# A transformer layer in fp32 on one core: the feed-forward taken for 512 tokens at once

## What is computed

```python
qkv = x @ Wqkv + bqkv                                # 256 -> 3 x 256
att = softmax(where(causal, q @ k.T * 16**-0.5, -inf))
x = layernorm(x + (att @ v) @ Wout + bout)
h = silu(x @ w1.T * w1_s) * (x @ w2.T * w2_s)        # 256 -> 1024
h = gelu(h @ h1.T * h1_s)                            # 1024 -> 1024
h = gelu(h @ h2.T * h2_s)                            # 1024 -> 1024
out = layernorm(x + h @ w3.T * w3_s)                 # 1024 -> 256
```

## Time and profile before

| what | value |
|---|---|
| median of 3 runs | 2513.91 us (2510.92 to 2515.61) |
| the profiled execution | 2513.84 us |
| its span, first to last instruction | 2512.1 us |
| TensorE busy | 2366.4 us (94%) |
| VectorE busy | 1264.6 us (50%) |
| ScalarE busy | 1335.7 us (53%) |
| GpSimd busy | 487.7 us (19%) |
| DMA moved | 183.35 MB, mean 73 GB/s |
| mean granted TensorE clock | 0.959 |

### The profile page before, as it was taken

How to read it: one execution, slowest core, us unless ns; L and a number is a source line. 1 busy time by engine, 2 the same in 40 slices (tenths; PEclk the granted TensorE clock), 3 DMA queues, 4 the chain that set the end, 5 groups by cost and what they waited for, 6 DMA issues and landing times.

```text
span 2512.1 us, 53072 instructions
## 1 busy us (share of the span) xinstructions
PE 2366.4 (94%) x16550; PEld 1834.4 (73%) x16550; DVE 1264.6 (50%) x3961; ACT 1335.7 (53%) x3104; POOL 487.7 (19%) x894
## 2 busy tenths in 40 slices
PE   5667999999999999999999999999999999999988
PEld 2225777777777777777777777777777777778788
DVE  2364454555545555554555555455555544555433
ACT  1334645555564655556465555646555564656543
POOL 0112212221220222122022212202221220222111
PEclk7557999999999999999999999999999999999999
DMA  4852122122222212112221211212121121212000
GB/s 153 295 184 64 53 68 76 51 86 61 60 68 63 81 52 85 61 54 75 62 82 52 85 60 54 75 62 82 52 85 54 60 75 59 85 52 65 13 5 9
DMA packets 109284, 183.35 MB, mean 73 GB/s; under 512 B 20608, under 2 KB 38784, under 8 KB 108928
## 3 DMA queue, kind: packets, MB, share of 16 engines
q1 hardware_dynamic: 109104, 180.70, 23.2%
HBM read 109.86 MB, written 72.88 MB: 73 GB/s over the span
## 4 chain that ended last, share of the span: by engine, by line
PE 75%; issue 6%; DVE 4%; ACT 3%; POOL 3%; POOLq 0%; ACTq 0%; DVEq 0%; SPq 0%; DMA 0%
PE ring L910 40%; PE ring L896 7%; PE pS L813 6%; PE ring L923 5%; PE pO L846 5%; PE pM L824 4%; PE ring L855 3%; PE ring L861 2%; POOL Xlo L486 2%; ACT probs L519 1%; PE ring L877 1%; POOL probs L480 1%; DVE pM L647 1%; ACT L574 1%; PE ring L885 1%
## 5 line engine op out<-in xcount | busy, mean ns | idle before, releaser
L647 DVE CUSTOM_DVE_ANT_0 pM<-pM,mask 128x512 f32<-128x512 f32 (+3 forms) x1024 | 491.9, 510 | 526.3 <-PE pM L824 431.9
L519 ACT ACTIVATE probs<-pS 128x512 f32<-128x512 f32 (+3 forms) x1024 | 392.1, 434 | 291.3 <-PE pS L813 288.3
L910 PE MATMUL ring<-Xhi,H 128*128 128x256 f32 x2048 | 528.0, 297 | 19.8 <-POOL Xlo L486 13.0
L910 PE MATMUL ring<-Yhi,H 128*128 128x256 f32 x2048 | 528.5, 296 | 0.0
L910 PE MATMUL ring<-Ylo,H 128*128 128x256 f32 x2048 | 504.3, 284 | 0.0
L910 PE MATMUL ring<-Xlo,H 128*128 128x256 f32 x2048 | 499.1, 282 | 0.0
L480 POOL TENSOR_SCALAR_AFFINE_SELECT probs<-probs 128x256 f32<-128x256 f32 x512 | 211.6, 413 | 1276.3 <-ACT probs L519 1272.3
L910 PEld LDWEIGHTS ring<-Xhi,H 128*128 128x128 f32 x2048 | 390.7, 191 | 46.6 <-ACT full_h L587 14.0
L910 PEld LDWEIGHTS ring<-Yhi,H 128*128 128x128 f32 x2048 | 394.5, 193 | 34.3 <-issue 21.0
L910 PEld LDWEIGHTS ring<-Ylo,H 128*128 128x128 f32 x2048 | 395.5, 193 | 0.0
L910 PEld LDWEIGHTS ring<-Xlo,H 128*128 128x128 f32 x2048 | 391.8, 191 | 4.4 <-issue 3.4
(11 more groups left out here) (88 smaller groups left out, 3026.5 us busy)
## 6 DMA issues: line engine op xcount, KB each, us to landing
Qs<-qk_d SPq DMA_DIRECT2D x64, 512.0 KB, 3.6
Ks<-qk_d SPq DMA_DIRECT2D x64, 512.0 KB, 4.5
qk_d<-c_hi SPq DMA_DIRECT2D x64, 256.0 KB, 2.4
qk_d<-c_hi SPq DMA_DIRECT2D x128, 128.0 KB, 2.4
qk_d<-c_lo SPq DMA_DIRECT2D x128, 128.0 KB, 2.4
xTs<-in_xT SPq DMA_DIRECT2D x16, 512.0 KB, 3.8
Oc<-Osb SPq DMA_DIRECT2D x256, 32.0 KB
xr<-in_x SPq DMA_DIRECT2D x16, 512.0 KB, 5.6
```

What stands on the lines that cost most here:

```text
L519: nc.scalar.activation(probs[:, e % NP_BUF, s, 0:n], pS[:, s, 0:n], ACT.Exp, scale=SCALE).then_inc(exp_done, 1)
L647: nc.vector.tensor_tensor_reduce(pM[:, s, 0:n], pM[:, s, 0:n], mask[:, T - n:T], 1.0, NEG, ALU.add, ALU.max, mx[:, t, 2 * p + s:2 * p + s ...
L910: mm = nc.tensor.matmul(to, w, x_part, start=(k == 0 and m == 0), stop=(k == KB - 1 and m == 1))
```

## The change

- The feed-forward takes all 512 tokens of an image at once. There are 8 `gu`, 8 `h1` and 8 `h2` units an iteration in place of 16 each, and their matmuls have 512 columns. A `gu` unit takes two ring banks (m = 0 gate, m = 1 up). `ffn_out` is still done in two halves.
- Xhi, Xlo, Yhi and Ylo double in size. To make room, H2 is no longer held whole: it is written once to DRAM in eight tiles (`h2_d`) and loaded each iteration, tile by tile, into three slots (`h2_load`, 512 KB each). x1Thi and x1Tlo lie over Yhi and Ylo, th over c_hi and c_lo, xr, x1 and z become one buffer xz for two images, and full_h is gone: the second gelu is written in place in PSUM.
- The low part of the gated product goes from GpSimd to VectorE.
- The list of steps is written anew: four table loads instead of eight, `qk` of the next image in exps(2), `h2` from unit 2 on after the last head group, `y` and `ln1` at the end of the same iteration. The loop on the hardware takes two iterations at a time.
- A ring bank of an h unit is now free after VectorE's subtraction (h_lo), not after ScalarE's second gelu (h_full).

```diff
     def exps(g, between):       # unchanged: exp of kt, p; steps "between"; pv(kt - 1)
+    def gated(j):
+        return [("gu", -1, (j,)), ("ffn_hi", -1, (j,))]
+    def hidden(layer, early, after):
+        for j in range(early):
+            steps.extend([("h_act", -1, (layer, j)), ("h_rest", -1, (layer, j))])
+        for j in range(early, KB):
+            add(layer, -1, j)
+            add("h_act", -1, layer, j)
+            steps.extend(after.get(j, []))
+            add("h_rest", -1, layer, j)
+            if layer == "h2" and j + H2_BUF < KB:
+                add("h2_load", -1, j + H2_BUF)
...
+    exps(1, {0: gated(4), 1: gated(5), 2: [m[0]], 3: gated(6) + [m[1]],
+             5: gated(7) + [m[2]], 6: [m[3]]})
...
+    exps(2, {0: [("qk", 1, (0,))], 1: [n[4]], 2: [n[5], ("qk", 1, (1,))], 3: [n[6]],
+             4: [n[7], split, ("qk", 1, (2,))], 6: [turn, ("qk", 1, (3,))]})
+    last_pv(2)
+    add("h2", -1, 0)
+    m = maxes(1, 0)
+    exps(3, {1: [m[0]], 2: [m[1]], 3: [m[2]], 4: [m[3]], 5: [m[4]], 6: [m[5]]})
+    add("h2", -1, 1)
     add("table", 0, "Gelu", 3)
+    last_pv(3)
+    add("h2_load", -1, 3)
+    add("h2_load", -1, 4)
+    split, turn = neg(1, 0)
+    n = maxes(1, 1)
+    hidden("h2", 2, {2: [("v", 1, (0,)), m[6], ("den", 0, ())],
+                     3: [("v", 1, (1,)), m[7], split, ("rec_save", 0, ())],
+                     4: [("v", 1, (2,)), turn, ("rec_load", 0, ())],
+                     5: [("v", 1, (3,)), n[0]],
+                     6: [n[1], ("den_turn", 0, ())],
+                     7: [("y", 0, (0,)), n[2], ("y", 0, (1,))]})
+    add("ln1_stats", 0)
+    add("ln1", 0)
...
+                    elif kind == "h2_load":
+                        j, = a
+                        slot = j % H2_BUF
+                        if j < H2_BUF:
+                            need(sp, h_ready, (b - 1) * UNITS + KB + H2_BUF * (H2_PER[slot] - 1) + slot + 1)
...
+                        else:
+                            sp.wait_ge(h_ready, b * UNITS + KB + j - H2_BUF + 1)
+                        held(sp)
+                        sp.dma_start(H2[:, slot].bitcast(F32), h2_d[j]).then_inc(h2_in[slot], 16)
...
-                    elif kind == "ffn_hi":
-                        half, j = a
-                        pool.wait_ge(x_hi, b * (2 * KB) + half * KB + j + 1)
-                        nc.gpsimd.tensor_tensor(Xlo[:, j], full_g[:, j % 2], Xhi[:, j].bitcast(F32),
-                                                ALU.subtract).then_inc(x_lo, 1)
...
+                    elif kind == "ffn_hi":
+                        j, = a
+                        dve.wait_ge(x_hi, b * KB + j + 1)
+                        nc.vector.tensor_tensor(Xlo[:, j], full_g[:, j % 2], Xhi[:, j].bitcast(F32),
+                                                ALU.subtract).then_inc(x_lo, 1)
...
-                "gu": lambda half, j: (ffn_full, 2 * KB, half * KB + j + 1),
-                "h1": lambda half, j: (h_full, 32, u_of("h1", half, j) + 1),
-                "h2": lambda half, j: (h_full, 32, u_of("h2", half, j) + 1),
-                "ffn_out": lambda half: (ln2, LN2, 6 * half + 1),
+                "gu": lambda j, m: (gated, KB, j + 1) if m else (ffn_full, KB, j + 1),
+                "h1": lambda j: (h_lo, UNITS, u_of("h1", j) + 1),
+                "h2": lambda j: (h_lo, UNITS, u_of("h2", j) + 1),
+                "ffn_out": lambda half: (ln2[half], LN2, 2),
...
+                        if kind == "h2":
+                            pe.wait_ge(h2_in[j % H2_BUF], 16 * (b * H2_PER[j % H2_BUF] + j // H2_BUF + 1))
```

More of the change, by code:

```diff
@@ L52 @@
 VW = D + 1
-NP_BUF = 4
 MISC = 3
+H2_BUF = 3
+H2_PER = [len(range(n, KB, H2_BUF)) for n in range(H2_BUF)]
 def plan_iteration():
@@ L81, in last_pv @@
         add("stack", 0 if g + 2 < NG else 1, (g + 2) % NG)
-    def hidden(layer, off, half, g, early, after):
-        if not early:
-            last_pv(g)
-            steps.extend(after.get(-1, []))
-        for j in range(early, KB):
-            add(layer, off, half, j)
-            waiting = [(layer, half, k) for k in range(early)] if j == early else []
-            for k, unit in enumerate(waiting):
-                steps.append(("h_act", off, unit))
-                if k == 0:
-                    last_pv(g)
-            if waiting:
-                steps.append(("h_rest", off, waiting.pop(0)))
-            add("h_act", off, layer, half, j)
-            steps.extend(after.get(j, []))
-            steps.extend(("h_rest", off, unit) for unit in waiting)
-            add("h_rest", off, layer, half, j)
@@ L104, in maxes @@
     def maxes(off, g):
         return [("max", off, (g, t, p)) for t in reversed(range(TB)) for p in range(PAIRS)]
-    def gated(off, half, at, others):
-        between = {e: list(more) for e, more in others.items()}
-        for e, n in at:
-            between.setdefault(e, []).append(("gu", off, (half, n)))
-            if n:
-                between.setdefault(e + (e == 6 and n == KB - 1), []).append(("ffn_hi", off, (half, n - 1)))
-        return between
-    m = maxes(0, 1)
-    add("table", 0, "Exp", 0)
@@ new lines, in plan_iteration @@
+    add("table", 0, "Exp", 0)
+    m = maxes(0, 1)
+    split, turn = neg(0, 1)
+    exps(0, {0: [("ffn_out", -2, (0,))],
+             1: [m[3], ("x1_turn", -1, (0,)), ("x1_turn", -1, (1,))],
+             2: [m[4], ("ffn_out", -2, (1,))],
+             3: [m[5], ("ln2_stats", -2, (0,))],
+             4: [m[6]] + gated(0) + [("ln2", -2, (0,))],
+             5: [m[7], split, ("load_xT", 1, ())],
+             6: gated(1) + [turn],
+             7: gated(2)})
+    last_pv(0)
+    steps.extend(gated(3))
@@ L670, in work @@
                     elif kind == "gu":
-                        half, j = a
-                        n = b * (2 * KB) + half * KB + j
-                        gate, up = (ring[:, BANKS[kind, off, a], m * HALF:(m + 1) * HALF] for m in range(2))
+                        j, = a
+                        n = b * KB + j
+                        gate, up = (ring[:, BANKS[kind, off, (j, m)]] for m in range(2))
+                        dve.wait_ge(gu_ready, 2 * n + 2)
+                        held(dve)
                         dve.wait_ge(tanh_done, n + 1)
@@ L784, in _, with iteration @@
             }
-            def iteration(i, steps, taken, general):
+            def iteration(i, steps, odd, taken, general):
                 def bank(kind, off, a):
```

337 lines of the change are left out of this document (161 added, 176 removed).

## The result

The changed kernel takes **3253.9 us** (median of 4 runs, 3248.2 to 3263.5) against 2513.1 for the kernel before on the same chip: ratio 1.295, interval 1.291 to 1.299. I had said 2820, range 2590 to 2960. Slower was right; the size was wrong by 434 us. The profiled execution has a span of 3246.8 us.

A forecast was written before the change was run, and what follows sets the result against it. TensorE's stream bounds the kernel; per iteration 12.1 us saved against 32.6 of waits, less 1.5 already there, gives +19.0 on 147.6. Over 15 iterations +285, +20 for the ends: 2513.8 becomes 2820 us, range 2590 to 2960.

The forecast's parts named there:

- The saving of wider matmuls: In h and gu units, 512-column matmuls at 216 ns take 12.1 us off an iteration of 147.6.
- rival D: Feed-forward matmuls of 512 columns take 240 ns, +92 us: 2910 us; chance 0.18 together with rival C.
- Wait 1: In exps(2), four c_hi in one phase each wait for the save before: 10.4 us an iteration, bounds 7.9 and 12.
- Wait 2: In exps(3), first maxima wait for the next image's Qs and Ks: 7.1 us with slower maxima, bounds 3 and 8.
- Wait 3: In h2, tile 3 of H2 is loaded late, behind a group's end and a stack: 5.0 us, bounds 3.5 and 6.
- Wait 4: Before h2 units 5 and 7, ring banks come free late: 1.0 and 2.7, together 3.7 us, bounds 2 and 5.
- Wait 5: In the gated product, VectorE's pace makes h1 unit 0 wait for the last Xlo: 6.4 us, bounds 0 and 10.
- rival C: Gaps also cost clock: h2 units 0 and 1 at half clock, 7 us an iteration, 2925 us; 0.18 together with D.
- the 1.5 that I had deducted: Per iteration, 1.5 us taken off the waits since some exist already in the 135.5: +20.5 becomes +19.0.
- the ends: First iterations (qk chain twice, H2 written in 512-byte pieces) and the last one: +20 us in all.
- A: TensorE's stream decides, waits fall where it has work queued: 2320 us; 0.11 including what lies up to no change.
- B: Only the waits in exps(2) and for the next image's stack are real: 2615 us; 0.21 with what lies between.

The follow-up runs named there:

- e11: Changed kernel with each 512-column matmul of the feed-forward's first three layers as two of 256, weights loaded twice: 3293.9 us, ratio 1.311.
- e1: Changed kernel with the four qk steps spread over h1 units 2 and 5, exps(2) and exps(3): 3170.9 us, ratio 1.261.
- e9: Changed kernel with the edits of e1, e2, e3 and e6 together, plus the Qs and Ks load ahead of a group's end: 2892.0 us, ratio 1.149.
- e5: Changed kernel with unused filler matmuls: 20 before the first maxima of exps(3), 26 before h2 unit 3, 12 before unit 7: 3222.0 us, ratio 1.284.
- e2: Changed kernel with H2's tile 3 load issued behind h2 unit 0 and tile 4's ahead of group 3's end: 3152.2 us, ratio 1.254.
- e3: Changed kernel with VectorE's subtraction of an h unit ahead of the steps behind that unit: 3211.1 us, ratio 1.277.
- e6: Changed kernel with the gated product's copy Xhi and low part one unit later, as in the kernel before: 3146.7 us, ratio 1.254.
- e13: Changed kernel with unused filler matmuls at two places only, 26 before h2 unit 3 and 7 before unit 7: 3221.9 us, ratio 1.282.
- e7: Changed kernel with the gated product's low part back on GpSimd, all else the same: 3221.9 us, ratio 1.283.

## Why the prediction was wrong, point by point

**What bounds, and the direction: right.** The list before hid its waits, the new one doesn't; in each of the five places that I named the trace shows one.

**The saving of wider matmuls: mis-sized.** I took 216 ns for 512 columns from the fp32 row; bounds 213 and 240. Here they start 235 ns apart on average at 2.4 GHz (median 228, over some 3270 pairs whose next is of the same line and within 600 ns), between my value and rival D's 240. An h unit with what parts it from the next instruction is 3.86 us, not 3.65, a gu unit 2.06, not 1.91: 16 x 0.21 + 8 x 0.15 = 4.6 us an iteration of the 12.1 were not there. The 256-column matmuls (120 ns) had told it: 13 ns beyond the columns, and 15 here with 512, are what the fp32r ones show, and I preferred a row of another type. The Trainium skill ("TensorE: Matmul & The Clock Gate", section Back-to-back issue gap) gives 2.5 ns beyond the columns and a sustained spacing of some 131 ns for 512 columns; neither is seen here in fp32r. e11 confirms that the wide form gains little.

**Wait 1: length right, value wrong.** From h1's last matmul to h2 unit 0 it is 24.4 us in the median (24.3 predicted), with c_hi's turn-round as its cause, and slow qk matmuls in it, which I hadn't. But I counted the wait against TensorE's own 13.9 us at full speed: TensorE is busy for 18.0 us of the phase, and with the waits gone and one qk in it the phase is still 15.1 us (e1), 12.3 of them busy. The whole of e1 gave 5.7 us.

**Wait 2: right.** TensorE waits 3.3 us by the profile before the first maxima in the iteration shown, and slow instructions, h2 unit 0 among them, fill most of the rest of the 5.3; e9 took 4.0 us an iteration off by moving the load ahead of those issues. The pairs behind it took 11.3 us (8.2 predicted); in e5, at 2.4 GHz, 8.5.

**Wait 3: too low.** 6.3 us in the median for 5.0 (beyond the upper bound of 6): H lands 6.0 us after its issue in the median of all tiles, this one with Qs, Ks and tile 4 beside it; I had 3.8 to 5.4. e2: 6.6 us back.

**Wait 4: right.** 1.0 and 2.7 us before units 5 and 7, as predicted; e3 took 1.8 of the second away.

**Wait 5: right to unit 0, then wrong.** The first unit's full_g was done 18.7 us after the end of y, as predicted; the seven others took 33.6 us in the median (36.4 in the iteration shown), not 28.7. I let VectorE's occupancy set the pace. What set it is ScalarE's copy Xhi at the head of its queue, waiting some 2 us each time for two of VectorE's instructions, with the exponentials behind it that TensorE's next scores need. I had costed the copy (0.58) and not what the new list does to it: before, it stood one unit later. In e6, with the copy back there, the seven units take 25.4 us, and the iteration 7.3 us less, more than the whole 6.4 that I had for wait 5. The 42.4 us of TensorE's work that I set against it stood in the sum without rows.

**The clock: the rival that should have been in the sum.** This is the step that failed most. The forecast put 32.6 us of gaps into a stream and left TensorE's own time at full speed; rival C stood apart with 0.18 for itself and D, and its 7 us had only h2 units 0 and 1. Over twelve steady iterations TensorE is busy for 161.7 us on average where my sum left 132.7, and 43.2 of them are at 1.2 GHz, which makes 21.6 us more than at 2.4. With the 4.6 of the spacing that is 26.2 of the 29.0 us; the idle time is 2.6 us under my sum. What these 21.6 us are worth in time is less certain. Where TensorE paces the kernel, h2 units 1, 3 and 7 are 4.7 us longer than at full speed and the pairs of exps(3) 2.7: e13 got two thirds back in units 3 and 7, e5 under half of what it removed, since filler also stands in the way. The Trainium skill ("TensorE: Matmul & The Clock Gate", section HAM oscillation — how this bites in real kernels) says that bursts with gaps between them fall back to the lower clock. The trace agrees: some 980 us of the span are at 1.2 GHz, and the matmuls that were 0.23 us apart ahead of the 6.7 us gap are 0.43 apart behind it. The gap of the earlier trace rows, which I took for agreement in the prediction, did not show it: the clock was at the lower level already in the stretch before that gap.
```profile
208.00:214.00 6.00, 3.98 (x20) 2.26 (x16) 3.85 (x19) 1.42 (x3) 0.95 (x1) 0.50 0.12 27
```

**The account.** The period is 193.4 us, my forecast 147.6 + 19.0 = 166.6: 26.8 apart. Spacing 4.6; gated product 3.7 (33.6 less 28.7, less the spacing in it); slow stretches in exps(3) and h2 at most 7.4; wait 3 another 1.3; the 1.5 that I had deducted as "already there", 1.5; the low clock of h1 unit 0 about 1, which e7 took away. Together 19 to 20 at the most. The remaining 7 us an iteration have no experiment, and their cause stays open. 26.8 x 15 = 402 us of the 434. The other 32 lie in the ends, which I had at 20: between the profiled executions the first two iterations differ by 15 us more than two steady ones do, and the stretch from the last iteration's first table load to the end is 27 us longer than before. The causes weren't looked into.

**Rivals.** A (no wait counts, 2320) and B (2615) are out: each wait named is in the trace. The spacing lies about midway between my value and D's. C had the right mechanism, in too few places. C, half of D, and e6's mechanism, which no rival had, are the parts of the miss that the runs show.
